# One recurrent step of a fused kernel: gate o gets a bank and an activation of its own, and 1 + o moves to VectorE

## The reference

```python
def step(carry, xs):
    h, c = carry
    xi_t, xf_t, xg_t, xo_t = xs
    i_t = jax.nn.sigmoid(xi_t + h @ V_i)
    g_t = jnp.tanh(xg_t + h @ V_c)
    o_t = jax.nn.sigmoid(xo_t + h @ V_o)
    c_new = h * c + i_t * g_t
    h_new = o_t * jnp.tanh(c_new)
    return ((h_new, c_new), h_new)
```

## Time and profile before

| | |
|---|---|
| median of three runs | 4057.43 us |
| profiled execution, its own time | 4055.54 us |
| its span, first to last instruction | 4053.8 us |
| PE busy | 3656.8 us, 90% |
| DVE busy | 3421.4 us, 84% |
| ACT busy | 2616.3 us, 65% |
| GpSimd busy | 2157.9 us, 53% |
| granted TensorE clock, mean | 0.517 of full speed |

### The profile page before, as it was taken

The page is one execution under the profiler, slowest core; times in us unless marked ns, Lnnn a source line. Parts: engine busy times, 40 slices in busy tenths (PEclk is TensorE's granted clock), DMA queues, the critical chain, the costliest instruction groups (busy, mean ns, idle before and its releaser), DMA issues.

```text
span 4053.8 us, 134735 instructions
## 1 busy us (share of the span) xinstructions
PE 3656.8 (90%) x35548; PEld 2705.8 (67%) x35548; DVE 3421.4 (84%) x21829; ACT 2616.3 (65%) x11666; POOL 2157.9 (53%) x3173
## 2 busy tenths in 40 slices
PE   6799999999999999999999999999989999988888
PEld 5666666666666666666666666666666666666665
DVE  6788888888888888888888888888888888887787
ACT  3366666666666666666666666666666666666665
POOL 6655555556555556555555555555655555652222
PEclk7955555555555555555555555555555555555555
DMA  5000000000000000000000000000000000000000
GB/s 73 2 1 1 1 1 1 1 1 1 1 1 1 1 1 1 1 1 1 1 1 1 1 1 1 1 1 1 1 1 1 1 1 1 1 2 1 1 1 1
DMA packets 44537, 11.06 MB, mean 3 GB/s; under 512 B 39913, under 2 KB 44010, under 8 KB 44490
## 3 DMA queue, kind: packets, MB, share of 16 engines
q1 hardware_dynamic: 42378, 10.05, 1.6%
q10 hardware_dynamic: 2112, 0.46, 0.1%
HBM read 7.29 MB, written 3.21 MB: 3 GB/s over the span
## 4 chain that ended last, share of the span: by engine, by line
PE 66%; DVE 14%; ACT 13%; issue 5%; POOL 1%; DMA 0%; DVEq 0%; ACTq 0%; POOLq 0%
PE GATES L1272 13%; PE YB L1092 9%; PE GATES L1289 8%; ACT O L703 7%; PE H1B L1086 7%; PE TAPB L1079 7%; ACT G L700 6%; DVE O L919 6%; PE YB L1243 6%; PE DB L1211 5%; DVE HR L923 5%; PE DB L1073 3%; PE H1B L1119 1%; PE H2B L1119 1%; PE H2B L1067 1%
## 5 line engine op out<-in xcount | busy, mean ns | idle before, releaser
L700 ACT ACTIVATE G<-GATES 128x12 f32<-128x12 f32 x3136 | 574.2, 183 | 1172.7 <-PE GATES L1289 1121.9
L914 DVE TENSOR_TENSOR_SCAN CT<-G,CT 128x12 f32<-128x12 f32 x3136 | 587.4, 187 | 274.9 <-ACT G L700 249.9
L1289 PEld LDWEIGHTS GATES<-HR,VW 128*128 128x128 f16 x6272 | 431.7, 108 | 569.9 <-issue 532.9
L1272 PE MATMUL GATES<-HR,VW 128*128 128x4 f16 x3136 | 549.8, 175 | 285.6 <-DVE HR L923 208.2
L703 ACT ACTIVATE O<-G 128x8 f32<-128x8 f32 x3136 | 668.6, 213 | 100.4 <-ACT G L700 0.2
L919 DVE RECIPROCAL O<-O 128x4 f32<-128x4 f32 x3136 | 567.5, 181 | 178.0 <-ACT O L703 1.0
L1285 PEld LDWEIGHTS <-VW 128*128 128x128 f16 x3136 | 457.6, 146 | 346.0 <-issue 309.7
L925 DVE TENSOR_TENSOR_SCAN H<-O,CT 128x24 f16<-128x24 f32 x3136 | 615.3, 196 | 0.0
L930 DVE SCALAR_TENSOR_TENSOR CT<-HIST,CT 128x4 f32<-128x4 f32 x3136 | 521.6, 166 | 108.8
L1289 PE MATMUL GATES<-H,VB 128*128 128x4 f16 x6272 | 611.6, 168 | 0.0
L1289 PE MATMUL GATES<-HR,VW 128*128 128x4 f16 x6272 | 610.4, 168 | 0.0
(11 more groups left out here) (243 smaller groups left out, 7021.4 us busy)
## 6 DMA issues: line engine op xcount, KB each, us to landing
out_dram<-OUT SPq DMA_DIRECT2D x112, 28.0 KB, 1.9
X<-in_x_dram SPq DMA_DIRECT2D x4, 672.0 KB, 11.3
STG<-in_L_ffn_w_dram SPq DMA_DIRECT2D x4, 512.0 KB, 12.7
U<-in_L_conv_U2s_dram SPq DMA_DIRECT2D x1, 972.0 KB
W<-in_L_ffn_w_dram SPq DMA_DIRECT2D x1, 512.0 KB, 12.0
X<-in_x_dram ACTq DMA_DIRECT2D x4, 112.0 KB, 3.3
S<-in_L_conv_S1s_dram SPq DMA_DIRECT2D x1, 108.0 KB
S<-in_L_conv_S2s_dram SPq DMA_DIRECT2D x1, 108.0 KB
```

Of the source, the lines that this page charges most:

```text
L700: act.activation(G6[:, :, 2:5], gates[c][:, w, :, :], ACT.Tanh, scale=1 / GSCALE).then_inc(step_in, 1)
L914: dve.tensor_tensor_scan(CELL.rearrange("z b k -> z (b k)"), G6[:, :, :].rearrange("z b k -> z (b k)")[:, 0::2], ADD3.rearrange("z b k -> ...
L1272: return pe.add_instruction(mybir.InstMatmult(name=nc.get_next_instruction_name(), engine=mybir.EngineType.PE, start_tensor_calc=False, st ...
L1289: last = pe.matmul(gates[c][:, w, :, SLOT[g]], wt[:, g].rearrange("z m c -> z (m c)"), digit, start=False, stop=True, skip_group_check=True)
```

## The change

The gates i and g stay in their bank; gate o goes into a bank of its own, which is the old bank DB. What used DB moves: the norms' spread to H2B, the expert weights to H1B, with other waits for that. A step's products are reordered so that o's comes last for HR and for H5; the semaphore gates_done is set after the second product with VB, gate_o_done after the third. ACT makes a tanh of 8 columns (i, g) and then one of 4 (o, into OT). VectorE computes 1 + o from OT by a scalar_tensor_tensor with two copies in the output, in front of the reciprocal; HSCALE moves into HR, and O5, H5 and TC5 have 5 elements per image instead of 6. The bank of o is shared with no start flag any more, so ACT zeroes the other half of it at steps 1 and 49, and the three input products of o come last and wait for that step's tanh of o. Waited values, and addresses, are computed ahead by `pe_registers`, `act_registers` and a longer `fill_registers`; the first value of a row on VectorE is kept in a register.

```diff
-GRID = 0.75
+GRID = 1.5 * 2.0 ** 13
-        PRE0={51: (0, 1, 2), 52: (3, 4), 53: (5, 6), 54: (7, 8)}, ...)
+        PRE0={51: (0, 1), 52: (2, 3), 53: (4, 5), 54: (6, 7, 8)}, ...)
-PRE1_AT = {3: (0, 1, 2, 3, 4), 6: (5, 6, 7, 8)}
-SLOT = (2, 0, 1)
+INPUTS = (("b", 0), ("b", 1), (0, 0), (0, 1), (1, 0), (1, 1), ("b", 2), (0, 2), (1, 2))
+FIRST_O = INPUTS.index(("b", 2))
+PRE1_AT = {3: (0, 1, 2, 3, 4, 5), 6: (6, 7, 8)}
+ZERO_AT = (1, 49)
+SLOT = (1, 0)
@@ banks
+        GATE_O = [DB[:, c * TOK:(c + 1) * TOK] for c in range(2)]
+        gate_o = [g.rearrange("z (b t) -> z t b", b=B) for g in GATE_O]
         def spread(lstm):
-            return DB if lstm else GATES[1]
+            return H2B if lstm else GATES[1]
+        def weights_bank(lstm):
+            return H1B if lstm else DB
@@ act_row
-                    act.activation(G6[:, :, 2:5], gates[c][:, w, :, :], ACT.Tanh, scale=1 / GSCALE).then_inc(step_in, 1)
-                    act.wait_ge(step_in, 1 + 2 * n + 2)
-                    act.activation(O5[:, :, 1:5:3], G6[:, :, 3:4].broadcast_to([128, B, 2]), ACT.Copy, scale=O_MAX * HSCALE, bias=HSCALE)\
-                        .then_inc(o1_done, 1)
+                    act.activation(G6[:, :, 2:5:2], gates[c][:, w, :, :], ACT.Tanh, scale=1 / GSCALE).then_inc(step_in, 1)
+                    act.wait_ge(gate_o_done, 1 + n + 1)
+                    act.activation(OT[:, :], gate_o[c][:, w, :], ACT.Tanh, scale=1 / GSCALE).then_inc(ot_done, 1)
+                    act_registers(act, j, t, involution)
                     act.wait_ge(cell_done, 1 + n + 1)
...
+                    for k in range(2):
+                        if t == ZERO_AT[k]:
+                            act.activation(GATE_O[1 - k], CST[:, CZERO:CZERO + 1].broadcast_to([128, TOK]), ACT.Copy).then_inc(oz_done, 1)
@@ dve_row
-                    dve.wait_ge(step_in, 1 + 2 * n + 2)
+                    dve.wait_ge(step_in, first if t == 0 else 1 + 2 * n + 2)
                     dve.tensor_tensor_scan(CELL...)
                     fill_registers(dve, j, t, involution, lstm, experts)
+                    dve.wait_ge(ot_done, 1 + n + 1)
+                    dve.scalar_tensor_tensor(out=O5[:, :, 1:5:3], in0=OT[:, :].unsqueeze(2).broadcast_to([128, B, 2]), scalar=O_MAX,
+                                             in1=O5[:, :, 2:3].broadcast_to([128, B, 2]), op0=ALU.mult, op1=ALU.subtract)\
+                        .then_inc(o1_done, 1)
                     dve.wait_ge(o1_done, 1 + n + 1)
                     dve.reciprocal(O5[:, :, 3], O5[:, :, 1]).then_inc(rec_done, 1)
                     dve.wait_ge(t_done, 1 + n + 1)
-                    dve.tensor_tensor(HR[:, :], O5[:, :, 1], TC5[:, :, 0], ALU.mult).then_inc(hd1_done, 1)
+                    dve.scalar_tensor_tensor(out=HR[:, :], in0=O5[:, :, 1], scalar=HSCALE, in1=TC5[:, :, 0], ...)
@@ fill_registers: also the values at GAT, XC, LG, DPLO, OUT_FREE_AT, OUT2, OUT3, MAX, IDX, and
-                    dve.to_reg(window(j, k, 2 * h, 2).offset)
+                    dve.lower_ap(window(j, k, 2 * h, 2))
@@ pe_fill
+                    if k == FIRST_O:
+                        pe.wait_ge(ot_done, 1 + (j - LAG) * W + t + 1)
...
-                pe.wait_ge(si_done, 1 + NG * j + k)
+                if lstm:
+                    pe.wait_ge(dbs_done, 1 + NG * j + k)
@@ pe_row
-                        for g in range(1, 3):
-                            last = pe.matmul(gates[c][:, w, :, SLOT[g]], wt[:, g]..., digit, start=False, stop=True, ...)
-                    last.then_inc(gates_done, 1)
+                        last = pe.matmul(gates[c][:, w, :, SLOT[1]], wt[:, 1]..., digit, start=False, stop=True, ...)
+                        if wt is VB:
+                            last.then_inc(gates_done, 1)
+                        if wt is VW and t - 1 in ZERO_AT:
+                            pe.wait_ge(oz_done, 1 + 2 * (j - LAG) + ZERO_AT.index(t - 1) + 1)
+                        last = pe.matmul(gate_o[c][:, w, :], wt[:, 2]..., digit, start=False, stop=True, ...)
+                    last.then_inc(gate_o_done, 1)
```

## The result

The kernel after takes 4456.43 us (median of 4, 4453.88 to 4458.28), the kernel before 4057.48 (median of 4, 4057.04 to 4061.83; the 4057.43 shown ahead is of three of them): ratio 1.098, 95% interval 1.0961 to 1.0999. The forecast was 4150, its range ended at 4200. The sign was right, and so was the path on which the time is lost. The size was not: of 399 us lost, 93 were forecast, and most of the rest comes from a wait that the forecast doesn't have.

The account below looks back on a forecast made before the run. Bound: a chain of waits, PE, ACT and DVE taking turns around one recurrence. Rows of 69.79 + 0.70 = 70.49 us against 68.79 add 94 us to 4055.5: forecast 4150 us, range 4040 to 4200.

Parts of the forecast that it names:

- the term D: Duration of VectorE's STT for 1 + o, on the chain: taken as 155 ns, bounds 131 and 170.
- second price: Skill's measured price for an STT like 1 + o: (N + 151)/0.96, 166 ns; result would be 34 us above the forecast.
- first price: Skill's price for an STT like 1 + o: 58 cycles plus elements at 0.96 GHz, 69 ns; ruled out by HIST.
- F: Register run between cell scan and STT, which starts 60 + F behind the scan; 57 to 123 ns, median 65.
- steps 8 and 12: Single places in a row where the STT comes late: 0.10 us more lost in each.
- the row's start: Head of each row on VectorE: 120 ns lost before the change, 110 after.
- VectorE's own loop: ADD3, VV and next scan on VectorE, deciding 26 of a row's 56 steps: 1257 ns a step.
- (d): Fills start sooner, as PE, ACT and DVE no longer compute waited values before them: 0.6 us a row gained.
- step 6: Place in a row where o's first input product waits for that step's tanh of o: VB products 0.28 us late.
- 1: Rival: register runs cost the STT nothing, it starts 95 ns behind the scan: 125 us less, 4025; 9%.
- 2: Rival: register runs free and STT at most 145 ns, o's path off the chain: 85 us less, 3970; 9%.
- 3 (D = 131): Rival: a short STT of 131 ns on VectorE: 75 us less; 10%.

Follow-up runs that it names:

- experiments 4: Kernel before with two more VectorE STTs per step, each with one input in PSUM, into a scratch tile: 4192.06 us.
- experiment 1: Kernel after with OT, the tanh of o, in PSUM instead of SBUF: 4286.34 us.
- experiment 3: Kernel before with one more VectorE STT per step behind ADD3, both inputs in SBUF, output read by nobody: 4368.7 us.
- experiment 9: Kernel after with VectorE's register block moved behind HIST: 4279.00 us with 1 + o by tensor_scalar, 4070.31 us with the tanh of o in PSUM.

## Why the prediction was wrong, step by step

**What failed first is the term D**, "Duration D of the STT, eight elements SBUF to SBUF ... Bounds 131 and 170; I take 155". It has two errors.

The smaller one is the STT's own time. Undisturbed the STT takes 169, the upper bound's side: 14 x 3136 = 44 us. The second price that the prediction quotes from the Trainium skill ("VectorE: DVE Perf Modes", the section on the TRN2 errata) gives an estimate of 166, and this trace agrees with it within 3 ns; started closer behind another instruction, as in experiments 4 and 9, the STT takes 157 to 159. (The prediction set HIST's 133 ns against the first price; HIST has an operand in PSUM and can't decide that, the 168 ns can.)

The larger error is that no wait for GpSimd was in the sum, and none in the range. The bounds of D came from rows in which VectorE had no rival: the nearest forms had an operand in PSUM, and the one row from SBUF to SBUF is one of two setup instructions. Such a wait was put at nothing, and it measured 181 us (experiment 1 takes it away, experiment 3 brings it about in the kernel before). The prediction said of GpSimd only that nothing in its queue is changed. True, and no evidence: the new instruction meets that queue. I never asked which of the loop's VectorE instructions read nothing but SBUF. The recurrence has the reciprocal alone; outside it there is for one DM's tensor_scalar, and its row in the trace of the kernel before had the warning (min/median/max):

```profile
L865 DVE TENSOR_SCALAR DM<-IOT,IXF,PW x248: 280/289/541, 19.1 to 3992.2; 112x16 f32<-112x16 f32 x124
```

58 of them last over 300 ns, 56 of these once a row: 0.38 to 0.40 us in 50 rows and 0.53 to 0.54 in the last six. All 56 began while GpSimd's RSE ran, and end 27 to 30 ns behind it.

**Second, F in product steps**: "F 80 to 111, mean 88, and 10 for the full address". The address did not lengthen the run, it became a second one, and two runs put the STT 225 to 270 ns behind the scan instead of 158: 54 us. From the scan to the STT all steps together take 506 us; by the forecast's 124, 129 and 158 it is 420. Some 10 of the 86 us belong to steps 8 and 12, which were counted elsewhere, and 9 to step 0: 76 us without 8 and 12. The rule 60 + F itself is right within 1 ns for one run (118 to 137 ns for 57 to 76).

**Third, the row's start**: "110 after (the branch's run is gone, three registers more in F)". The scan stands 1289 ns behind G (median) against 332: 48 us in 50 rows. Nothing in the forecast looked at the length of a loop body.

**What was too dear**: VectorE's own loop at 1257 in 26 steps. The scan comes 212 to 213 behind G there as elsewhere; VV lets it in after 0.33 us, not 0.366, so the loop over G decides (1239 to 1252) and 44 us of the forecast were not there. That this just makes up for the 44 us of the undisturbed STT is luck. The forecast span is 4053.8 + 94 = 4148 us, and 4148 + 44 + 181 + 76 + 48 - 44 = 4453 of the profiled span of 4456; the rest I don't assign.

**What was right**: o's path is last everywhere; G 26 + 4 ns sooner; tanh of o at G + 73; 34 to the reciprocal, 216 (217) to H5, 481 to the next G (480); (d); step 12 1333 - 1239 = 94 ns (100); step 8 a further 0.1 us; step 6 at 1433 (near 1.5 us) and step 54 0.05. Step 12, with its STT 219 ns behind the scan, is worth 94 x 56 = 5 us (6).

**The rivals.** 1 and 2 (register runs cost nothing) are refuted by an STT 118 to 270 ns behind the scan, against 96 in experiment 9, where the block is moved; 3 (D = 131) by the least that any STT of this form took, 168 ns in the kernel after and 154 in all runs. The real one, that the new instruction meets GpSimd's and waits for it, was not among them, and I gave 72% to a sum whose bounds were drawn from undisturbed rows.

**Left open**: why the stall (median from branch to hint) is 0.52 to 0.65 us in four kernels and 0.81, 1.06 and 1.24 in three others, although six of the seven have bodies of 1076 or 1077; by what condition the tensor_scalar is held and the reciprocal not; what makes GpSimd's RS_Y no holder; whether steps 6 and 54 can be mended, which wasn't tried.

## What to carry to other kernels

Before an operation goes to VectorE beside a busy GpSimd, list where each operand lies: if all its inputs lie in SBUF it may wait for what GpSimd is doing, and a row of a form with one PSUM operand is no bound for it. The mean in the group's row hides this; min/median/max (168/169/796) shows it at once. On a chain whose links last 200 ns, count register runs as instructions, two runs as two, and look at what stands directly in front of the link. Keep an eye on an unrolled body's length, since two instructions more per step can cost a refetch in each turn.

## What the runs showed of the hardware that I had not expected

- An STT or tensor_scalar from SBUF of 8 elements a partition lasted up to 948 and 916 ns (157 to 174 undisturbed) beside GpSimd's tensor_tensor and copy instructions, and the long ones nearly always ended 13 to 35 ns behind one of these; beside RS_Y none was long. The same STT with one input in PSUM ran in 157 to 163 ns 1262 times while GpSimd was working, the reciprocal of the kernel after in 180 to 185.
- A VectorE loop body of 1021 instructions or more was read anew in each row (about 5 packets, 40 KB), one of 965 was not; the engine stood 0.52 to 1.24 us in the median, against 0.26.
- A register run of 37 ns in front of an ACT copy made it start 82 ns later (355 against 273 behind G), 240 us over the kernel.
